# Seven buffers instead of three for the streamed hypernet matrices, and a later read-back of the first half

## The chip, the core and the metric

One core of a Trainium2 chip runs the whole program. The time is the device time of one execution in microseconds (us); the reported figure is the median of several executions. TensorE (PE in the rows) multiplies matrices, VectorE (DVE) and ScalarE (ACT) do elementwise work, GpSimd (POOL) clears memory and issues transfers here, and SyncE (SP) only issues transfers. All transfers are carried by the same 16 DMA engines, whichever engine issues them.

## What is computed

Four layers are applied to `x` (4 batches, 512 tokens, 256 features), each steered by a condition vector of 64 numbers for each batch. The second one, which the change touches, builds its weights for each batch from the condition:

```python
# layer 0: layer norm, plus tanh(cond @ lin_w.T + lin_b)
# layer 1: adapter whose weights come out of a hypernet
dWd = ((h_lang @ Wdd.T + bdd) * 0.1).reshape(B, BN, D)      # Wdd is (128*256, 64)
dWu = ((h_lang @ Wdu.T + bdu) * 0.1).reshape(B, D, BN)      # Wdu is (256*128, 64)
down = relu(einsum('bld,bnd->bln', x, Wd + dWd) + bd)
x = x + einsum('bln,bdn->bld', down, Wu + dWu) + bu
# layer 2: rms norm, up projection 256 -> 2*1024, gelu gate,
#          int8-like activations times ternary weights, residual
# layer 3: attention with 16 heads of 16, then a gated MLP 256 -> 1024 -> 256
```

`Wdd` and `Wdu` are 8 MiB each. They are read once and are by far the largest inputs.

## The kernel before

The program has a prologue, then one long body for each of the four batches. The body holds layers 2 and 3 of its batch and, tucked into its last part, layers 0 and 1 of the next. The prologue does the hypernet for all four batches together, and layers 0 and 1 of batch 0.

**The stream.** The two hypernet matrices come as 32 pieces of 512 KiB (`load(p)`, issued by SP at L268), pieces 0 to 15 from `Wdd` and 16 to 31 from `Wdu`. A piece goes into one of `PIECES` = 3 buffers in `arena`, buffer `p % 3`. Before piece p is issued, SP waits until TensorE has consumed piece p - 3 (`e_piece`). TensorE takes two pieces for each step n of 0 to 15 (`hyp(n)`, L1057, four matmuls a piece, each shown as two instructions). ScalarE scales the result of a step out of PSUM (`hyp(n)`, L452), and every second step stores it to a scratch tensor `hyp_out` in HBM (`store`, L443). `hyp(n)` on TensorE waits for ScalarE's copy of step n - 3.

**The read-back.** The result must be laid out anew, so it is fetched from `hyp_out` into `hypw`: `fetch(0)` (L279, the result of pieces 0 to 15) and `fetch(1)` (L285, pieces 16 to 31). SP issues `fetch(0)` inside the stream, right after `load(22)` (`p == 2 * (AT_DOWN - 1)` with `AT_DOWN` = 12), once the stores of pieces 0 to 15 have landed; `fetch(1)` comes after `load(31)`, when all stores have landed. VectorE adds the static weights and splits the sum into two parts (`first_weights(m)`, L774 add, L776 cast, L728 subtract).

**What sits between the pieces.** Every engine works in program order. Steps n carry other prologue work, at the same n on each engine: `parameters` after n = 1 (L1040 on TensorE), `deviation`/`front_stats`/`front_norm` at 3, `front_turn` at 4 (L1081), `weight_sum` at 6 (L1047), `first_weights(0)` at `AT_DOWN` - 1, `front_down` and `front_bottleneck` at `AT_DOWN` (six matmuls at L1071 that need `fetch(0)`). After the last piece: `first_weights(1)`, `front_up` (L1071), and then batch 0.

**GpSimd.** It clears two of the three stacked query tiles (`qst[0]`, `qst[1]`, L378) and other tiles at the start, then issues ten loads of split weights (`load_stage`, L400, 256 KiB each), four at once and each later one when VectorE has worked off the load four places before. When all pieces are consumed and all stores have landed it issues the twelve late loads (`gh_w`, `out_w`) in the same manner. `POOL_READY` = 6 counts its early clears. The query tiles are first written in the attention of batch 0, by transfers that SP issues in `stack_q`.

Of the kernel before, what the change touches and what calls it, by code (L numbers as in the profile page):

```python
# [20 lines left out]
F32 = mybir.dt.float32  # L21
# [7 lines left out]
P = 128  # L29
# [9 lines left out]
G = 4  # L39
# [13 lines left out]

HP = 8
HALF_PIECE = 256
PIECES = 3
STAGES = 4
SLOT = 2
HALF = L // 2
# [10 lines left out]
def build(nc, x, cond_t, cond_blk, vec_w, alpha_w, vecs, out_b, hyp_base, hyp_bias, hyp_w,  # L70
          up_w, down_w, qk_w, vo_w, gh_w, out_w, out):
    ctx = ExitStack()
    with ctx:
        def sb(name, shape, dt=F32):
            return ctx.enter_context(nc.sbuf_tensor(name, shape, dt))

        def sem(name):
            return ctx.enter_context(nc.semaphore(name))
# [39 lines left out]


        kst = [sb(f"kst{i}", [P, G // 2, L], F32R) for i in range(3)]  # L120
        qst = [sb(f"qst{i}", [P, G, L], F32R) for i in range(2)] + [act_both]
        inp = kst[0:2]
        vals = sb("vals", [P, T, NH, VW])
# [39 lines left out]
        oT = cut(6144, 1024, c=C, n=L)  # L163
        tmpz = fT.rearrange("p c n -> p (c n)").rearrange("p (t d) -> p t d", t=T)

        piece = cut(0, 3072, r=PIECES, g=4, n=HALF_PIECE)
        vecw_in = [x2T[0:CND, 0, :], x2T[0:CND, 1, :], vow[0:CND, 1, :]]
        down_in = hypw[:, :, :].rearrange("p b n -> p (b n)")
        bias_in = vow[:, 0, :]
# [20 lines left out]
        keys_lo_in = sem("keys_lo_in")  # L190
        keys_in = [sem(f"keys_in{i}") for i in range(3)]
        hblk_set = sem("hblk_set")
        act_zero, keys_ones = sem("act_zero"), sem("keys_ones")
        rows_in, out_done = sem("rows_in"), sem("out_done")
        pool_ready = sem("pool_ready")
# [56 lines left out]
        NPIECE = 2 * HP  # L252
        HYP_BANK = (1, 2, 7)

        AT_PARAMS, AT_STATS, AT_TURN, AT_WSUM, AT_DOWN = 1, 3, 4, 6, 12
        SMALL = 4

        block = ctx.enter_context(nc.Block())
# [2 lines left out]
        @block.sync  # L261
        def _(sp):
            def load(p):

                m, s, col = p // (2 * HP), p % (2 * HP) // 2, p % 2 * HALF_PIECE
                if p >= PIECES:
                    sp.wait_ge(e_piece, p - PIECES + 1)
                sp.dma_start(piece[:, p % PIECES, :, :],  # L268
                             hyp_w[m].rearrange("p (g s n) -> p g s n", g=4, s=HP)[:, :, s, col:col + HALF_PIECE]
                             ).then_inc(piece_in[p % PIECES], 16)  # L270

            def fetch(m):

                for hf in range(2):
                    sp.wait_ge(hyp_stored[hf], 16 * 4 * (m + 1) * HP // SLOT // 2)
                if m == 0:
                    sp.wait_ge(d_downq, 1)
                    for r in range(C):
                        sp.dma_start(hypw[:, :, r * BN:(r + 1) * BN],  # L279
                                     hyp_out[0, 4 * r:4 * r + 4, :].rearrange("b (p n) -> p b n", p=P)  # L280
                                     ).then_inc(hyp_moved, 16)
                else:
                    for first, last, moved in ((0, 1, hyp_moved), (1, B, hyp_rest)):
                        for r in range(2):
                            sp.dma_start(hypw[CND * r:CND * r + CND, first:last, D:2 * D],  # L285
                                         hyp_out[1, 4 * r + first:4 * r + last, :]
                                         .rearrange("b (p n) -> p b n", p=CND)).then_inc(moved, 16)

            sp.dma_start(hblk[:, 0:8], cond_blk).then_inc(hblk_in, 16)
            load(0)  # L290
            sp.dma_start(condT[:, :], cond_t).then_inc(params_in, 16)
            sp.dma_start(vec[:, :], vecs).then_inc(params_in, 16)
            for i in range(3):
                sp.dma_start(vecw_in[i], vec_w[:, 512 * i:512 * i + 512]).then_inc(params_in, 16)
            for p in range(1, 2 * NPIECE):
                load(p)
                if p == 2:
                    sp.dma_start(x_tok[:, :, :], x[0:L, :].rearrange("(t p) d -> p t d", p=P)
                                 ).then_inc(x_first, 16)
                if p == 4:  # L300
                    sp.dma_start(alpha[:, :], hyp_base).then_inc(small_in, 16)
                    sp.dma_start(bias_in, hyp_bias).then_inc(small_in, 16)
                if p == 6:
                    sp.dma_start(down_in, down_w).then_inc(down_sem, 16)
                if p == 8:
                    sp.dma_start(alphaw[:, :], alpha_w).then_inc(small_in, 16)
                    sp.dma_start(outb[:, :], out_b.partition_broadcast(P)).then_inc(small_in, 16)
                if p == 2 * (AT_DOWN - 1):
                    fetch(0)
            fetch(1)  # L310
            sp.wait_ge(d_base, 1)
            sp.wait_ge(e_prm, 1)
            sp.dma_start(vow[:, :, :], vo_w).then_inc(vow_in, 16)

            def stack_q(b, g):

                if g >= 3:
                    sp.wait_ge(e_score, b * (NG * T * G) + T * G * (g - 2))  # L320
                if g == 2:
                    sp.wait_ge(act_zero, b + 1)
                for e in range(2):
                    for k, part in enumerate((0, 1, 0)):
                        src = split[32 * g + DH * e:32 * g + DH * e + DH, 4 * part:4 * part + 2, :]
                        dst = qst[g % 3][32 * k + DH * e:32 * k + DH * e + DH, e::2, :]
                        sp.dma_start(dst.bitcast(F32), src.bitcast(F32)).then_inc(queries_in[e][g % 3], 16)
                    if g == 0 and e == 0:
                        sp.wait_ge(a_qk, b * 4 + 4)
                        sp.wait_ge(d_qk, b * 4 + 4)  # L330
                        sp.dma_start(keys_of(0)[64:96, :, :].bitcast(F32), split[0:32, 6:8, :].bitcast(F32)
                                     ).then_inc(keys_lo_in, 16)

            def maxima_rows(b, g):

                for k, ready in enumerate((a_mrow, d_mrow)):
                    sp.wait_ge(ready, b * NG + g + 1)
                    dst = qst[g % 3][KROWS + k:KROWS + k + 1, :, :].rearrange("p i (t n) -> p (i t) n", t=T)
                    sp.dma_start(dst.bitcast(F32), mrow[k][:, :].bitcast(F32)).then_inc(rows_in, 16)

            def batch(b, last):
                if not last:
                    sp.wait_ge(d_x3, b * T + T)
                    sp.dma_start(x_tok[:, :, :], x[bass.ds(b * L + L, L), :].rearrange("(t p) d -> p t d", p=P)
                                 ).then_inc(x_in, 16)
                sp.wait_ge(a_qk, b * 4 + 2)
                sp.wait_ge(d_qk, b * 4 + 2)
                for g in range(3):
                    stack_q(b, g)
                maxima_rows(b, 0)  # L350
                maxima_rows(b, 1)
                stack_q(b, 3)
                maxima_rows(b, 2)
                maxima_rows(b, 3)
                for h in range(2):
                    sp.wait_ge(d_outs, b * 2 + h + 1)
                    sp.dma_start(out[bass.ds(b * L + h * HALF, HALF), :].rearrange("(t p) d -> p t d", p=P),
                                 x4_tok[:, 2 * h:2 * h + 2, :]).then_inc(out_done, 16)

            with sp.Fori(0, B - 1) as b:  # L360
                batch(b, False)
            batch(B - 1, True)
            sp.wait_ge(out_done, 32 * B + 32)


        POOL_READY = 6

        @block.gpsimd
        def _(pool):
# [4 lines left out]
            for m in (ident, ident16):  # L374
                pool.affine_select(out=m[:, :], in_=m[:, :], compare_op=ALU.not_equal, fill=1.0, base=0,
                                   pattern=[[-1, P]], channel_multiplier=1).then_inc(pool_ready, 1)
            for i in range(2):
                pool.memset(qst[i][:, :, :].bitcast(F32), 0.0).then_inc(pool_ready, 1)  # L378
            pool.memset(kst[2][:, :, :].bitcast(F32), 1.0).then_inc(pool_ready, 1)
            pool.memset(vals[:, :, :, :], 1.0).then_inc(pool_ready, 1)  # L380

# [24 lines left out]
            pool.wait_ge(e_piece, 2 * NPIECE)  # L406
            for n in range(LATE, NSPLIT):
                load_stage(n)
            pool.wait_ge(pool_ready, POOL_READY)
            with pool.Fori(0, B) as b:  # L410
                pool.wait_ge(e_vg, b * 8 + 1)
# [622 lines left out]
        def _(pe):  # L1034
# [14 lines left out]
            def hyp(n):  # L1049

                if n >= 3:
                    pe.wait_ge(a_hyp, n - 2)
                for p in (2 * n, 2 * n + 1):
                    pe.wait_ge(piece_in[p % PIECES], 16 * (p // PIECES + 1))
                    col = p % 2 * HALF_PIECE
                    for g in range(4):
                        ins = pe.matmul(bank[HYP_BANK[n % 3]][32 * g:32 * g + 32, col:col + HALF_PIECE],  # L1057
                                        hblk[:, :], piece[:, p % PIECES, g, :], start=True, stop=True,
                                        tile_position=(0, 32 * g))
                    ins.then_inc(e_piece, 1)  # L1060

# [396 lines left out]
```

## Time and profile before

| | us |
|---|---|
| three executions | 771.07, 772.25, 770.39 |
| their median | 771.07 |
| profiled execution, first to last instruction | 773.6 |
| start of the last piece's matmuls | 84.29 |
| start of `front_up` | 95.21 |
| TensorE busy in the whole span | 658.1 |
| VectorE / ScalarE / GpSimd busy | 431.5 / 381.9 / 55.0 |

The profiled execution is one execution of its own; the page gives its span and no other time for it. The prologue is the first eighth of the span. In it the DMA engines are the busy resource; after it TensorE is. The profile is read from the prologue alone, since all that the change touches lies there, except a wait in `stack_q`.

### The profile page before, as it was taken

The page shows a single profiled execution, that of the slowest core. Times are in us where ns is not written, and L with a number is a line of the kernel's source. Part 1 is how long each engine was busy: PE and PEld are TensorE (multiplying, and loading weights), DVE is VectorE, ACT ScalarE, POOL GpSimd, SP SyncE. Part 2 cuts the span into 40 slices and gives each one's busy share as a digit, 9 for nine tenths or more (in the row PEclk, how much of TensorE's full clock was granted, in tenths as well). Part 3 has the DMA queues.
Part 4 walks back from the last instruction along what each step waited for, and adds up shares of the span by engine and source line. Part 5 has one row for each costly group of instructions (what it writes and reads, how often), then busy time and mean ns, then how long its engine had stood idle before and what let it go on. Part 6 is the DMA issues. An engine that isn't in the chain of part 4 may idle for free.

```text
span 773.6 us, 9912 instructions
## 1 busy us (share of the span) xinstructions
PE 658.1 (85%) x3426; PEld 436.7 (56%) x3426; DVE 431.5 (56%) x863; ACT 381.9 (49%) x729; POOL 55.0 (7%) x91
## 2 busy tenths in 40 slices
PE   2655289699989998799989998799899996999896
PEld 0411176554448876455468876354488765544585
DVE  0352078397536565588255575787165663984344
ACT  1333077426773446246863447067752554267710
POOL 4010111200000000200000000200000002000000
PEclk9755689859999999769999999689989999599999
DMA  8898521422000000502000001510000002220000
GB/s 264 292 296 285 171 87 54 95 57 44 2 1 1 1 28 28 113 13 43 2 2 1 1 28 33 118 33 11 0 0 0 14 14 62 61 44 2 1 1 28
DMA packets 34473, 44.97 MB, mean 58 GB/s; under 512 B 4736, under 2 KB 27392, under 8 KB 34304
## 3 DMA queue, kind: packets, MB, share of 16 engines
q1 hardware_dynamic: 30048, 31.87, 14.8%
q0 software_dynamic: 3872, 11.54, 5.6%
q10 hardware_dynamic: 512, 1.05, 0.4%
q8 instruction: 21, 0.34, 0.2%
q14 instruction: 20, 0.16, 0.1%
HBM read 28.45 MB, written 3.15 MB: 41 GB/s over the span
## 4 chain that ended last, share of the span: by engine, by line
PE 70%; DMA 11%; ACT 8%; DVE 6%; issue 2%; SPq 2%; ACTq 0%
PE psum L1071 31%; PE psum L1237 12%; PE psum L1257 8%; PE psum L1266 8%; DMA arena<-in_hyp_w 7%; DMA kst<-split 2%; PE psum L1057 2%; PE psum L1294 1%; DMA qst<-mrow_lo 1%; ACT arena L473 1%; ACT arena L613 1%; PE psum L1159 1%; PE psum L1090 1%; PE psum L1199 1%; PE psum L1144 1%
## 5 line engine op out<-in xcount | busy, mean ns | idle before, releaser
L916 DVE TENSOR_REDUCE mx<-psum 128x1 f32<-128x512 f32 x256 | 160.9, 683 | 48.8 <-PE psum L1237 48.4
L613 ACT ACTIVATE arena<-psum 128x512 f32<-128x512 f32 x256 | 140.8, 601 | 67.0 <-PE psum L1257 66.0
L1237 PE MATMUL psum<-kst,qst 96*128 96x512 f32 x192 | 102.9, 623 | 22.5 <-DMA kst<-split 20.7
L1071 PE MATMUL psum<-act,ghw_hi 128*128 128x512 f32 (+1 forms) x288 | 93.6, 394 | 0.5 <-DVE act L728 0.2
L1237 PEld LDWEIGHTS psum<-kst,qst 96*128 96x128 f32 x192 | 49.7, 261 | 72.4 <-DVE mx L916 41.1
L1257 PE MATMUL psum<-qst,kst 98*128 98x512 f32 x192 | 83.4, 454 | 3.6 <-DMA qst<-mrow_lo 1.8
L1071 PE MATMUL psum<-upw_hi,kst 128*128 128x512 f32 x256 | 72.2, 404 | 0.0
L1057 PE MATMUL psum<-arena,hblk 128*32 128x256 f32 x256 | 31.0, 579 | 44.3 <-DMA arena<-in_hyp_w 42.4
L1266 PE MATMUL psum<-arena,vals 128*17 128x512 f32 x512 | 67.4, 598 | 1.3 <-ACT arena L613 1.0
L1071 PEld LDWEIGHTS psum<-act,ghw_hi 128*128 128x128 f32 x288 | 56.7, 208 | 11.3 <-DVE act L728 1.7
L639 ACT ACTIVATE arena<-psum 128x512 f32<-128x512 f32 x32 | 19.2, 599 | 85.0 <-PE psum L1071 85.0
L1071 PE MATMUL psum<-act,ghw_lo 128*128 128x512 f32 (+1 forms) x144 | 55.8, 389 | 0.0
L968 DVE TENSOR_TENSOR arena<-arena,psum 128x512 f32<-128x512 f32 x32 | 22.0, 687 | 59.1 <-ACT arena L639 59.1
L1257 PEld LDWEIGHTS psum<-qst,kst 98*128 98x128 f32 x192 | 39.0, 208 | 25.5 <-ACT arena L613 16.3
L1071 PEld LDWEIGHTS psum<-upw_hi,kst 128*128 128x128 f32 x256 | 47.0, 191 | 9.6
L1071 PE MATMUL psum<-outw_hi,split 128*128 128x256 f32 x256 | 47.4, 283 | 1.2 <-DVE split L728 1.2
L551 ACT ACTIVATE arena<-psum,stat 128x512 f32<-128x512 f32 x32 | 21.9, 686 | 44.8 <-PE psum L1071 44.8
L1057 PEld LDWEIGHTS psum<-arena,hblk 128*32 128x32 f32 x256 | 6.8, 135 | 65.5 <-DMA arena<-in_hyp_w 38.3
L1071 PEld LDWEIGHTS psum<-outw_hi,split 128*128 128x128 f32 x256 | 41.2, 188 | 4.6 <-DVE split L728 2.1
L390 POOL DMA_DIRECT2D kst<-split x44 | 21.3, 490 | 273.4 <-ACT split L577 154.7
L1071 PE MATMUL psum<-upw_lo,kst 128*128 128x512 f32 x128 | 40.2, 395 | 0.0
L928 DVE RECIPROCAL rden<-psum 128x16 f32<-128x16 f32 (+1 forms) x20 | 4.7, 234 | 59.5 <-PE psum L1278 59.5
(162 smaller groups left out, 1025.2 us busy)
## 6 DMA issues: line engine op xcount, KB each, us to landing
arena<-in_hyp_w SPq DMA_DIRECT2D x32, 512.0 KB, 5.2
kst<-split POOLq DMA_DIRECT2D x44, 128.0 KB, 4.0
qst<-split SPq DMA_DIRECT2D x72, 64.0 KB, 3.4
arena<-in_x SPq DMA_DIRECT2D x4, 512.0 KB, 3.5
arena<-in_up_w POOLq DMA_DIRECT2D x8, 256.0 KB, 7.7
arena<-in_gh_w POOLq DMA_DIRECT2D x8, 256.0 KB, 3.8
out_x<-arena SPq DMA_DIRECT2D x8, 256.0 KB, 2.1
act<-split SPq DMA_DIRECT2D x24, 64.0 KB, 2.3
```

What stands on the lines that cost most here:

```text
L390: pool.dma_start(keys_of(g)[32 * k:32 * k + 32, :, :].bitcast(F32), src.bitcast(F32)).then_inc(keys_in[g % 3], 16)
L473: s.activation(to, src(c), ACT.Identity, scale=scale, bias=prm[:, col_b + c:col_b + c + 1]).then_inc(signal, 1)
L551: s.activation(gl[:, n % 2, :], bank[2 * (n % 2) + 1], ACT.Gelu, scale=stat[:, RS2, t:t + 1]).then_inc(a_gelu, 1)
L613: s.activation(probs[:, kb % 2, i, :], bank[3 + n % RING], ACT.Exp).then_inc(a_p, 1)
L639: s.activation(sg[:, f % 2, :], bank[2 * (f % 2)], ACT.Silu).then_inc(a_silu, 1)
L916: v.reduce_max(mx[:, g % 2, col:col + 1], bank[u % RING], AX.X).then_inc(d_max, 1)
L968: v.tensor_tensor(hh[:, f % 2, :], sg[:, f % 2, :], bank[2 * (f % 2) + 1], ALU.mult).then_inc(d_hh, 1)
L1057: ins = pe.matmul(bank[HYP_BANK[n % 3]][32 * g:32 * g + 32, col:col + HALF_PIECE], hblk[:, :], piece[:, p % PIECES, g, :], start=True, sto ...
L1071: ins = pe.matmul(dst, lhs(a, c), rhs(z, c), start=start and n == 0, stop=stop and n == len(terms) - 1, skip_group_check=skip)
L1237: pe.matmul(bank[u % RING], qst[g % 3][0:KROWS, i, P * t:P * t + P], keys_of(g)[0:KROWS, i // 2, :], start=True, stop=True).then_inc(e_max, 1)
L1257: pe.matmul(bank[3 + k % RING], keys_of(g)[0:SROWS, i // 2, P * kb:P * kb + P], qst[g % 3][0:SROWS, i, :], start=True, stop=True).then_inc ...
L1266: ins = pe.matmul(bank[6][32 * i:32 * i + VW, :], vals[:, kb, G * g + i, :], probs[:, kb % 2, i, :], start=(kb == 0), stop=(kb == T - 1), ...
```

## The change

The ring of piece buffers grows from 3 to 7. Three stay where they were, in `arena`. The other four lie in a tensor `early_pieces` whose memory is given back at once and is then allocated again as `qst[0]` and `qst[1]`. These two tiles can therefore be cleared only after the last piece is consumed: GpSimd clears them after the fourth late weight load, a new semaphore `queries_zero` tells SP, and `stack_q` waits for it before the first stacked queries of each batch. `AT_DOWN` goes from 12 to 13, and `fetch(0)` is issued after `load(24)`.

```diff
-PIECES = 3
+PIECES = 7
+ARENA_PIECES = 3
...
+        with nc.sbuf_tensor("early_pieces", [P, 2 * G * L], F32) as early_pieces:
+            pass
         qst = [sb(f"qst{i}", [P, G, L], F32R) for i in range(2)] + [act_both]
...
-        piece = cut(0, 3072, r=PIECES, g=4, n=HALF_PIECE)
+        arena_piece = cut(0, 1024 * ARENA_PIECES, r=ARENA_PIECES, g=4, n=HALF_PIECE)
+        early_piece = early_pieces[:, :].rearrange("p (r g n) -> p r g n", g=4, n=HALF_PIECE)
+
+        def piece(p):
+            r = p % PIECES
+            return arena_piece[:, r, :, :] if r < ARENA_PIECES else early_piece[:, r - ARENA_PIECES, :, :]
...
-        AT_PARAMS, AT_STATS, AT_TURN, AT_WSUM, AT_DOWN = 1, 3, 4, 6, 12
+        AT_PARAMS, AT_STATS, AT_TURN, AT_WSUM, AT_DOWN = 1, 3, 4, 6, 13
...
                 if p >= PIECES:
                     sp.wait_ge(e_piece, p - PIECES + 1)
-                sp.dma_start(piece[:, p % PIECES, :, :],
+                sp.dma_start(piece(p),
...
-                if p == 2 * (AT_DOWN - 1):
+                if p == 24:
                     fetch(0)
...
+                if g == 0:
+                    sp.wait_ge(queries_zero, 2)
                 if g >= 3:
                     sp.wait_ge(e_score, b * (NG * T * G) + T * G * (g - 2))
...
-        POOL_READY = 6
+        POOL_READY = 4
...
-            for i in range(2):
-                pool.memset(qst[i][:, :, :].bitcast(F32), 0.0).then_inc(pool_ready, 1)
             pool.memset(kst[2][:, :, :].bitcast(F32), 1.0).then_inc(pool_ready, 1)
...
             for n in range(LATE, NSPLIT):
                 load_stage(n)
+                if n == LATE + STAGES - 1:
+                    for i in range(2):
+                        pool.memset(qst[i][:, :, :].bitcast(F32), 0.0).then_inc(queries_zero, 1)
```

How the instructions stand. SP, from the ninth piece to the last transfer of the prologue (`in_hyp_w` is a piece, `hypw<-hyp_out 128x4x128` is `fetch(0)`). Before:

```order
L306 DMA alphaw<-in_alpha_w 64x512
L307 DMA outb<-in_out_b 128x256
L268 DMA arena<-in_hyp_w 128x4x256 x14
L279 DMA hypw<-hyp_out 128x4x128 x2
L268 DMA arena<-in_hyp_w 128x4x256 x9
L285 DMA hypw<-hyp_out 64x256 x2
L285 DMA hypw<-hyp_out 64x3x256 x2
L313 DMA vow<-in_vo_w 128x1024
```

After:

```order
L278 DMA arena<-in_hyp_w 128x4x256
L278 DMA early_pieces<-in_hyp_w 128x4x256 x4
L278 DMA arena<-in_hyp_w 128x4x256 x3
L278 DMA early_pieces<-in_hyp_w 128x4x256 x4
L278 DMA arena<-in_hyp_w 128x4x256 x3
L278 DMA early_pieces<-in_hyp_w 128x4x256
L289 DMA hypw<-hyp_out 128x4x128 x2
L278 DMA early_pieces<-in_hyp_w 128x4x256 x3
L278 DMA arena<-in_hyp_w 128x4x256 x3
L278 DMA early_pieces<-in_hyp_w 128x4x256
L295 DMA hypw<-hyp_out 64x256 x2
L295 DMA hypw<-hyp_out 64x3x256 x2
```

Nine pieces stood behind `fetch(0)`, and seven stand there now.

TensorE, from the pieces behind `front_turn` to `front_up` (`kst,split` x6 is `front_down`, `split` x6 is `front_up`; a piece is `x4`). Before:

```order
L1057 MATMUL psum<-arena,hblk 32x256 x16
L1047 MATMUL psum<-wstat,alpha_ob 128x1
L1057 MATMUL psum<-arena,hblk 32x256 x48
L1071 MATMUL psum<-kst,split 128x512 x6
L1057 MATMUL psum<-arena,hblk 32x256 x24
L1071 MATMUL psum<-split 128x512 x6
```

After:

```order
L1070 MATMUL psum<-early_pieces,hblk 32x256 x16
L1060 MATMUL psum<-wstat,alpha_ob 128x1
L1070 MATMUL psum<-arena,hblk 32x256 x12
L1070 MATMUL psum<-early_pieces,hblk 32x256 x16
L1070 MATMUL psum<-arena,hblk 32x256 x12
L1070 MATMUL psum<-early_pieces,hblk 32x256 x16
L1084 MATMUL psum<-kst,split 128x512 x6
L1070 MATMUL psum<-arena,hblk 32x256 x12
L1070 MATMUL psum<-early_pieces,hblk 32x256 x4
L1084 MATMUL psum<-split 128x512 x6
```

Six pieces stood behind `front_down`, and four stand there now.

GpSimd, from its early clears to the last late load. Before:

```order
L378 MEMSET qst 128x2048 x2
L379 MEMSET kst 128x1024
L380 MEMSET vals 128x1088
L400 DMA arena<-in_up_w 128x512 x8
L400 DMA arena<-in_qk_w 128x512 x2
L400 DMA arena<-in_gh_w 128x512 x8
L400 DMA arena<-in_out_w 128x512 x4
```

After:

```order
L389 MEMSET kst 128x1024
L390 MEMSET vals 128x1088
L410 DMA arena<-in_up_w 128x512 x8
L410 DMA arena<-in_qk_w 128x512 x2
L410 DMA arena<-in_gh_w 128x512 x4
L421 MEMSET qst 128x2048 x2
L410 DMA arena<-in_gh_w 128x512 x4
L410 DMA arena<-in_out_w 128x512 x4
```

The two clears moved from the front of the queue to behind the fourth late load.

## Rows read from the trace of the kernel before

**Rows 1.** The head of the page: the span.
```profile
span 773.6 us, 9912 instructions
```

**Rows 2.** Windows: length, busy us (instructions) by engine, clock, DMA share, GB/s.
```profile
7.00:25.00 18.00, 9.04 (x56) 6.20 (x60) 0.09 (x1) 2.90 (x5) 2.49 (x5) 1.00 1.01 343
25.00:28.00 3.00, 2.13 (x20) 0.59 (x12) 2.43 (x16) 1.11 (x2) 0.00 (x0) 1.00 0.45 145
28.00:36.00 8.00, 2.11 (x20) 0.59 (x24) 4.14 (x17) 2.70 (x4) 0.54 (x1) 0.68 0.97 329
36.00:42.00 6.00, 4.76 (x36) 2.08 (x32) 2.52 (x5) 4.50 (x7) 0.54 (x1) 0.58 0.72 237
42.00:51.00 9.00, 3.67 (x34) 0.96 (x33) 7.53 (x9) 2.34 (x4) 2.48 (x3) 0.64 1.02 329
51.00:61.00 10.00, 5.40 (x40) 1.10 (x40) 0.69 (x1) 1.74 (x4) 0.54 (x1) 0.50 0.78 247
61.00:70.00 9.00, 3.51 (x28) 0.86 (x32) 2.53 (x5) 2.28 (x4) 0.00 (x0) 0.50 1.03 336
70.00:72.00 2.00, 1.50 (x16) 0.20 (x8) 0.00 (x0) 0.32 (x2) 0.00 (x0) 0.50 0.66 179
76.00:84.00 8.00, 2.76 (x32) 0.60 (x28) 1.29 (x2) 2.16 (x4) 0.00 (x0) 0.88 0.71 232
```

**Rows 3.** Waits of SP's queue up to 100 us: total us, times, longest.
```profile
SPq L268 <- PE psum L1057: 48.1, 24, 6.0
```

**Rows 4.** Timeline: start, us, engine; three pieces of TensorE's other work between the pieces.
```profile
19.13 3.58 PE L1040 MATMUL psum<-condT,arena 64*128 64x4 f32 x16
...
36.62 1.97 PE L1081 MATMUL psum<-ident,arena 128*128 128x128 f32 x8
...
72.33 2.93 PE L1071 MATMUL psum<-kst,split 128*128 128x512 f32 x6
```

**Rows 5.** Timeline: piece 15, the stores behind it, and `fetch(0)`.
```profile
47.27 1.08 PE L1057 MATMUL psum<-arena,hblk 128*32 128x256 f32 x8 [0.49 <-DMA arena<-in_hyp_w]
...
49.05 1.32 ACTq L443 DMA_DIRECT2D hyp_out<-arena  x4
...
58.76 1.95 SPq L279 DMA_DIRECT2D hypw<-hyp_out  x2
```

**Rows 6.** The chain that ended last, in order of time: piece 28, piece 31 to `front_up`.
```profile
77.58 0.67 PE psum L1057 x8
...
84.29 1.12 PE psum L1057 x8
...
87.06 2.06 DMA hyp_out<-arena
...
89.71 4.21 DMA hypw<-hyp_out
...
94.40 0.30 DVE split L776
...
95.21 2.94 PE psum L1071 x6
```

**Rows 7.** Timeline: GpSimd's clears and loads, and a VectorE pass beside one.
```profile
1.88 3.54 POOL L378 MEMSET qst<- 128x2048 f32 x2
...
46.46 1.41 POOL L400 DMA_DIRECT2D arena<-in_qk_w  x1 [0.76 <-DVE upw_lo L725]
46.47 1.29 DVE L701 TENSOR_SCALAR hypw<-hypw,wstat 128x2048 f32<-128x2048 f32 x1
...
89.65 2.12 POOL L400 DMA_DIRECT2D arena<-in_gh_w  x4 [31.56 <-DMA hyp_out<-arena]
```

**Rows 8.** Instructions that write or read `hypw`: times; min/median/max ns; forms.
```profile
L728 DVE TENSOR_TENSOR split<-hypw,split x5: 426/692/693, 67.8 to 575.7; 128x512 fp32r<-128x512 f32 x3, 128x256 fp32r<-128x256 f32 x2
...
L765 DVE CAST split<-hypw x3: 420/423/423, 239.5 to 575.2; 128x512 fp32r x2, 128x512 fp32r<-128x512 f32 x1
```

**Rows 9.** Transfers by issue, whole span: number, KB each, median us to landing.
```profile
arena<-in_up_w POOLq DMA_DIRECT2D x8, 256.0 KB, 7.7
```

More of the change, by code:

```diff
@@ L192, in build @@
         hblk_set = sem("hblk_set")
+        queries_zero = sem("queries_zero")
         act_zero, keys_ones = sem("act_zero"), sem("keys_ones")
@@ L1057, in hyp @@
                         ins = pe.matmul(bank[HYP_BANK[n % 3]][32 * g:32 * g + 32, col:col + HALF_PIECE],
-                                        hblk[:, :], piece[:, p % PIECES, g, :], start=True, stop=True,
+                                        hblk[:, :], piece(p)[:, g, :], start=True, stop=True,
                                         tile_position=(0, 32 * g))
```

## The prediction

> **What bounds the kernel now.** The change lives in the prologue, so I read the chain of waits from `front_up` backwards, then the windows over the stream, then what TensorE did in each window where the DMA engines were not full.
>
> The chain [rows 6] shows a fixed tail. The last piece's matmuls start at 84.29, its copy is stored (the store lands after 2.06 us), `fetch(1)` takes 4.21 us, and `front_up` starts at 95.21. The tail of 95.21 - 84.29 = 10.9 us contains no choice that the ring of buffers could touch; it follows wherever the last piece lands. Everything behind `front_up` (batch 0, the late loads, the other batches) starts from it. So the question is only when piece 31 lands.
>
> The windows [rows 2] tell what paces the stream. The DMA engines have two kinds of stretches. In 7:25, 28:36, 42:51 and 61:70 they are full (share 0.97 to 1.03) and move 329 to 343 GB/s. In 25:28, 36:42, 51:61, 70:72 and 76:84 they are partly empty (0.45, 0.72, 0.78, 0.66, 0.71) and move 145 to 247 GB/s. TensorE is busy for 3.51 of the 9 us in 61:70, with the DMA engines full, so it paces nothing by its own throughput. What it does is to hold buffers: SP's queue waited 48.1 us in 24 waits on TensorE's pieces [rows 3], so SP is nearly always waiting for a free buffer. Whenever TensorE turns to something else, at most two further pieces are in flight and the DMA engines run dry: the parameter matmuls from 19.13 (one of two groups, 3.58 us) stand ahead of 25:28, the transposes at 36.62 (1.97 us, and the wait for their input) in 36:42, and `front_down` at 72.33 (2.93 us) ahead of 76:84 [rows 4]. In 51:61 `fetch(0)`, issued at 58.76 [rows 5], stands in SP's queue between two pieces.
>
> **The change part by part.**
>
> *Seven buffers: the holes fill.* The five hollow stretches last 3 + 6 + 10 + 2 + 8 = 29 us. By bytes they moved 0.435 + 1.422 + 2.470 + 0.358 + 1.856 = 6.54 MB; at the 332 GB/s of the full stretches (between 329 and 336 [rows 2]; 7:25 holds other inputs too) that is 19.7 us, so 9.3 us go. By busy share they used 1.35 + 4.32 + 7.80 + 1.32 + 5.68 = 20.5 us, so 8.5 us go. I take 8.9 us, with both ends.
>
> Does a depth of seven really cover every hole? A piece takes 524 KB / 332 GB/s = 1.6 us of full DMA time, so seven stand for 11 us of work. The longest hold is the one at step 4, where TensorE waits for the normalised input and then transposes; it is no longer than the 6 us of the hollow stretch around it, 36:42 [rows 2]. The parameters hold it for about 5 us. Six us eat not quite four pieces, and three are still in flight: the cover holds, with some 5 us to spare.
>
> *A deeper queue does not cost rate.* In 7:25 the input x, the biases and GpSimd's first weight loads were queued beside the pieces, more than in any later stretch, and it was the fastest one (343 GB/s) [rows 2]. From there the cost is nothing; the bound on the other side is that 343 holds throughout, which is in the last rival.
>
> *`fetch(0)` after `load(24)`.* SP stops in it until the stores of pieces 0 to 15 have landed; queued behind it are loads 25 to 31. Piece 15 starts at 47.27 and its store is issued from 49.05 to 50.4 [rows 5]. When it lands there is not shown: 2.06 us later if it goes as the last store [rows 6], and no later than 58.76, when `fetch(0)` was issued. So SP is free between 5 and 11.5 us after piece 15's start. `load(24)` goes out when piece 17 is consumed, about 4 us after it; at that time pieces 18 to 24 are out, 11 us of work. Even the late end leaves about 3 us of queued pieces. Cost nothing; bound 1 us. The fetch then stands behind piece 24, and its reader `front_down` behind piece 27, three pieces or 4.8 us later, against about 1.2 us of VectorE work between: covered.
>
> *`front_down` after piece 27.* Its 2.93 us [rows 4] now come when four pieces are still to be taken. They land 1.6, 3.2, 4.8 and 6.4 us after piece 27, whether TensorE is busy or not. TensorE is back 4 us after piece 27 landed, and takes a piece in 0.67 us (piece 28, right after `front_down`) to 1.12 us (piece 31) [rows 6]. At 0.67 the backlog is gone when piece 31 lands; at 1.12 it ends 1.1 us late. I take 0.2.
>
> *GpSimd's clears leave the start.* Its first loads go out 3.5 us earlier [rows 7]. The DMA engines have spare share only before 7 us, some tenths of a us. I take it at nothing, gain bound 0.5.
>
> *The clears arrive at the tail.* GpSimd is released for the late loads with SP's `fetch(1)`: four issues from 89.65 last 2.12 us, to 91.8; two clears of 1.77 us each [rows 7] would stand at 91.8 to 95.3. The fifth late load waits for VectorE and went out far later, so no load is delayed. But VectorE's cast of the last weights starts at 94.40 [rows 6], in the second clear, on the tail. Do the two disturb each other? The trace has one such meeting: a load issue on GpSimd that takes 0.53 us elsewhere took 1.41 us beside a VectorE pass of 1.29 us, and ended just after it [rows 7]. That pass ran at 0.63 ns an element; the cast runs at 0.83 (423 ns for 512), where the subtraction takes 1.35 (692 ns) [rows 8]: both belong to the fast kind. No row shows a clear that starts first, so the bounds are 0 and 95.3 - 94.4 = 0.9 us. I take 0.9, since the nearest row shows that one waits for the other's end.
>
> The Trainium skill (SBUF — State Buffer, on the shared port pair) says that GpSimd and a VectorE copy or cast in its two-port mode exclude each other for whole instructions, whoever starts first. By that rule this is a cost of 0.9 us; without it the sum would be 0.9 us better. The trace agrees in the other order only (1.41 us in place of 0.53).
>
> *The wait on `queries_zero`.* Set at about 95 us, first asked for in the attention near 145: nothing.
>
> The sum: -8.9 + 0.2 + 0.9 = -7.8 us, nearly all of it before `front_up`. On the profiled span that is 773.6 [rows 1] to 765.8. The span lies 2.5 us above the median of the three executions; the edit is the same in both, so the forecast is 771.07 - 7.8 = 763.3 us, a gain of 1.0%.
>
> **The rivals.**
>
> *Only part of the holes closes* (something other than the buffers holds the stream). TensorE's step waits for ScalarE's copy three steps back, ScalarE in its order waits for the weight loads, and these took 7.7 us to land beside the stream [rows 9]. If more pieces ahead stretch them beyond the lead of four steps, some 18 us (16 steps in about 74 us), ScalarE holds TensorE and the ring fills up all the same. For it: the loads share the 16 engines. Against it: the 7.7 us were measured with the engines full most of the time. It would leave the holes of 36:42 and 51:61, or 1.7 + 2.2 us by share, so a gain of 7.8 - 3.9 = 3.9: 767.2 us.
>
> *The holes don't close at all* (the share dips because of small packets or HBM, not for lack of transfers). Then time stays at 771 plus or minus 1. Against it: each hole follows a hold of TensorE.
>
> *Slower: the read-back comes too late.* Stores on ScalarE's queue must get through beside seven pieces. If they land late, SP stands in `fetch(0)` with loads 25 to 31 behind it, and `front_down` on TensorE waits for the fetch with pieces 28 to 31 behind it. It starts to cost when the store behind piece 15 needs more than some 12 us (11 us of queued pieces), and each us more is a us. To eat the 7.8 us it must take over 20 us, where the trace bounds it by 9.7. At 24 us: 775 us.
>
> *More comes back*: the rate of 7:25 (343) holds through, no clash at the cast, 10.5 us: 760.6.
>
> **How the numbers follow.** The forecast of 763.3 with its ends (holes 8.5 to 9.3, cast 0 to 0.9, `front_down` 0 to 1.1, `fetch(0)` 0 to 1, start 0 to -0.5, and the drift of the rest of the program of about 1 us between executions) covers 761.2 to 766.5 and gets 0.67. More comes back 0.09. Part of the holes 0.13. Nothing 0.06. Slower 0.05. The range for 8 in 10 is 760.8 to 767.8. A measurement of this kernel tells about 0.2%, or 1.5 us, from no change. Faster by over 0.2%: 0.67 + 0.09 + 0.13 = 0.89, less a little for a partial gain under 1.5 us, 0.88. Within it 0.07. Slower 0.05.
>
> **What would show it.** In the profile of the changed kernel the windows up to the last piece should read 0.95 or more throughout, with SP's waits still long (the ring is full, not empty). The last piece's matmuls should start near 75.5 and `front_up` near 87.3. `fetch(0)` should be issued and no window behind it should dip. The cast of the second half should start late or stand beside the second clear. If the last piece is early but the time is not, something behind `front_up` took its place. If it is not early, look for who TensorE waited for in the stream: ScalarE's copies (first rival) or the fetch (third).

## Result and profile after

| | before | after |
|---|---|---|
| median of the executions, us | 770.73 (4) | 759.35 (4) |
| lowest to highest | 768.83 to 772.25 | 756.47 to 759.86 |
| ratio, 95% interval | | 0.9844 (0.9821 to 0.9868) |
| profiled span | 773.6 | 757.1 |
| last piece's matmuls start | 84.29 | 70.33 |
| `front_up` starts | 95.21 | 81.55 |

The change made the kernel 11.4 us faster by the medians, 12.0 by the ratio. The forecast was 763.3 us, a gain of 7.8, with a range of 760.8 to 767.8. The measured time lies below that range: the sign and the mechanism were right, the size was too small. The same kernel, measured twice more beside other experiments, came out at 0.9834 (0.9809 to 0.9858) and 0.9843 (0.9819 to 0.9867) of the kernel before.

First the windows over the stream, the counterpart of [rows 2]: length, busy us and instructions of TensorE, its weight loads, VectorE, ScalarE, GpSimd, then granted clock, DMA share and GB/s.

```profile
7.00:23.00 16.00, 8.71 (x52) 6.00 (x56) 0.00 (x0) 2.70 (x5) 0.00 (x0) 1.00 1.06 381
23.00:46.00 23.00, 14.86 (x114) 4.76 (x106) 16.71 (x43) 10.65 (x19) 3.56 (x5) 0.84 1.07 369
46.00:56.00 10.00, 6.25 (x48) 1.30 (x48) 2.08 (x3) 3.46 (x6) 0.54 (x1) 0.50 1.07 365
56.00:65.00 9.00, 4.74 (x40) 1.03 (x40) 2.44 (x5) 2.34 (x4) 0.00 (x0) 0.50 1.00 333
65.00:70.00 5.00, 5.00 (x34) 2.60 (x34) 0.00 (x0) 1.79 (x3) 0.00 (x0) 0.56 0.80 270
```

Two things are to be seen. The hollow stretches are gone: none of these windows up to 65 reads under 1.00, and in windows of 2 us between 8 and 68 the lowest share is 0.97. (In the two later profiles of the same kernel the lowest were 0.94 and 0.92, both at 62:64.) And the full stretches are fuller than before: 365 to 381 GB/s at a share of 1.06 to 1.07 up to 56 us, where the full stretches of before moved 329 to 343 at 0.97 to 1.03 [rows 2]. The second goes beyond the prediction, whose last rival had 343 throughout.

SP's queue waited far less for TensorE than in [rows 3] (48.1 us); instead its issues got longer. The row of the waits of SP's queue (total, times, longest), and the row of the pieces into the new memory (shortest, median, longest issue in ns), where the median before was 540:

```profile
SPq L278 <- PE psum L1070: 16.8, 18, 1.9
...
L278 SPq DMA_DIRECT2D early_pieces<-in_hyp_w x17: 546/1587/2438, 7.9 to 61.2; - x17
```

The chain that ended last, from `front_down` to `front_up`, answers to [rows 6]:

```profile
65.91 2.86 PE psum L1084 x6
68.77 2.22 PE psum L1070 x32
71.01 0.61 ACT arena L465
...
75.27 3.83 DMA hypw<-hyp_out
...
79.58 1.47 DVE split L789
...
81.55 2.94 PE psum L1084 x6
```

The tail keeps its length (70.33 to 81.55 is 11.2 us, before 10.9), but two of its steps are new in kind. The last four pieces (x32; the last of them from 70.33) run back to back right behind `front_down`: they had all but landed while TensorE was busy with it. And the cast at L789 takes 1.47 us in place of 0.30. The timeline shows what stands beside it:

```profile
75.21 2.12 POOL L410 DMA_DIRECT2D arena<-in_gh_w  x4 [24.99 <-DMA hyp_out<-arena]
...
77.32 3.56 POOL L421 MEMSET qst<- 128x2048 f32 x2
79.12 0.42 DVE L787 TENSOR_TENSOR hypw<-hypw,alpha 128x256 f32<-128x256 f32 x1 [8.35 <-DMA hypw<-hyp_out]
79.58 1.45 DVE L789 CAST split<-hypw 128x256 fp32r<-128x256 f32 x1
```

The second clear runs from 79.10 to 77.32 + 3.56 = 80.88, and the cast ends at 81.03. The add just before it (L787) also ran beside that clear, in its usual 0.42 us: only the cast was held up.

`front_up` starts 13.7 us earlier than before, while the medians differ by 11.4 and the two spans by 16.5. What lies behind `front_up` is the same work in both, and its length differs by some us from execution to execution: 678.4 us in the profile of before, 675.6 in that of after, 674.5 to 677.9 in the ten other profiles below. A span lies 1.8 us under the time of its execution in every run here, so the profiled execution of before took about 775.4 us, more than any of its times in the table. The pair of spans therefore overstates the gain, its 84.29 and 95.21 may be late as well, and the ratio of the times is the figure to keep. In two further profiles of the changed kernel `front_up` started at 82.02 and 83.17, 13.2 and 12.0 us earlier than in the one profile of before.

### The profile page after: what moved, and what is told of

The parts are those of the page before. It is cut to its first block, busy times and chain, and to the rows that moved or that the text cites. A ratio compares the mean times of both kernels' runs of the same rounds, so it can differ in the third digit from the quotient of the medians.

```text
span 757.1 us, 9912 instructions
## 1 busy us (share of the span) xinstructions
PE 655.9 (87%) x3426; PEld 434.2 (57%) x3426; DVE 432.2 (57%) x863; ACT 381.4 (50%) x729; POOL 55.0 (7%) x91
## 3 DMA queue, kind: packets, MB, share of 16 engines
q10 hardware_dynamic: 512, 1.05, 0.4%
## 4 chain that ended last, share of the span: by engine, by line
PE 69%; DMA 12%; ACT 8%; DVE 6%; SPq 3%; issue 2%; ACTq 0%
PE psum L1084 31%; PE psum L1250 12%; PE psum L1270 8%; PE psum L1279 8%; DMA early_pieces<-in_hyp_w 5%; DMA kst<-split 2%; PE psum L1307 1%; DMA qst<-split 1%; DMA arena<-in_hyp_w 1%; SPq L339 1%; DMA qst<-mrow_lo 1%; ACT arena L486 1%; ACT arena L626 1%; PE psum L1172 1%; PE psum L1103 1%
## 5 line engine op out<-in xcount | busy, mean ns | idle before, releaser
L929 DVE TENSOR_REDUCE mx<-psum 128x1 f32<-128x512 f32 x256 | 160.5, 681 | 48.1 <-PE psum L1250 47.6
L1084 PE MATMUL psum<-act,ghw_hi 128*128 128x512 f32 (+1 forms) x288 | 91.1, 386 | 1.2 <-DVE act L741 0.8
L1084 PEld LDWEIGHTS psum<-act,ghw_hi 128*128 128x128 f32 x288 | 54.6, 199 | 12.0 <-DVE act L741 2.5
L871 DVE SCALAR_TENSOR_TENSOR arena<-psum,stat,arena 128x512 f32<-128x512 f32 x32 | 23.9, 748 | 21.7 <-ACT arena L564 21.6
L1084 PE MATMUL psum<-outw_lo,split 128*128 128x256 f32 x128 | 36.1, 282 | 0.0
```

What stands on the lines that cost most here:

```text
L871: v.scalar_tensor_tensor(hbuf[:, t % 2, 512 * j:512 * j + 512], bank[2 * (n % 2)], stat[:, RS2, t:t + 1], gl[:, n % 2, :], ALU.mult, ALU.m ...
L929: v.reduce_max(mx[:, g % 2, col:col + 1], bank[u % RING], AX.X).then_inc(d_max, 1)
L1084: ins = pe.matmul(dst, lhs(a, c), rhs(z, c), start=start and n == 0, stop=stop and n == len(terms) - 1, skip_group_check=skip)
```

## Experiments

### What sets the rate: the stream alone

SP loads pieces and nothing else runs. The kernel leaves out the whole computation; its output is a copy of `x`.

```python
for d in (1, 2, 3, 4, 5, 7):                # buffers in the ring
    for p in range(16):
        if p >= d:
            sp.wait_ge(sems[d][p % d], 16 * (p // d))     # piece p - d has landed
        sp.dma_start(rings[d][:, p % d, :, :], <piece p>).then_inc(sems[d][p % d], 16)
    <wait until all have landed>
```

> This kernel computes nothing: SP alone loads pieces of the hypernet matrix, in six sections of 16 pieces, with rings of 1, 2, 3, 4, 5 and 7 buffers (tensors ring1 to ring7). A piece is issued when the piece that held its buffer before has landed; no engine reads them. The output is only a copy of x. Theory 'depth' (a deeper queue moves more bytes a second): about 4.0 us for a piece at depth 1 (130 GB/s), 2.1 at 2, 1.6 at 3 (330 GB/s), 1.45 at 4, 1.40 at 5 (375), and no more at 7. Rival 'other inputs' (the higher rate after the change comes from what runs beside the pieces or where they land): depths 3 to 7 all the same within 3%.

The windows inside the six sections, in the order of the depths (the last two numbers are DMA share and GB/s):

```profile
5.00:60.00 55.00, 0.00 (x0) 1.00 0.44 137
65.00:93.00 28.00, 0.00 (x0) 1.00 0.79 257
99.00:123.00 24.00, 0.00 (x0) 1.00 1.02 329
128.00:150.00 22.00, 0.00 (x0) 1.00 1.10 351
155.00:177.00 22.00, 0.00 (x0) 1.00 1.07 346
183.00:205.00 22.00, 0.00 (x0) 1.00 1.07 345
```

With three pieces out and no engine holding a buffer, the stream moves 329 GB/s at a share of 1.02. That is what the full stretches of the kernel before looked like. With four it moves 351 at 1.10, and five or seven bring no more. So a share of 1.0 is not the top: three transfers of 512 KiB keep the DMA engines short by some 6%. The expectation was right up to depth 4 and too high at five (375 against 346). The rival, no difference from 3 to 7, falls: 3 and 4 differ by 7%.

This leaves open why the changed kernel ran at 365 to 381.

### A second queue beside the stream

The same pieces, rings of 3 and of 7, each once alone and once with GpSimd loading ten 256 KiB weight tiles beside them. Again nothing is computed.

```python
SECTIONS = ((3, 0), (3, 10), (7, 0), (7, 10))     # (buffers, weight loads on GpSimd)
pool.dma_start(side[k][:, p % 4, :], up_w[:, c, n:n + 512])     # four in flight
```

> Computes nothing, output a copy of x: four sections of 16 pieces by SP alone, ring of 3 buffers, ring of 3 with GpSimd loading ten 256 KiB weight tiles (2 KiB runs) beside it, ring of 7, ring of 7 with the same loads. stream_alone levelled off at 345 to 351 GB/s from depth 4, while the changed kernel ran at 365 to 381. Theory 'several queues': a second issuing queue raises the level, 365 to 380 GB/s at depth 7 with the loads, 345 to 350 without; at depth 3, 330 without and 345 or more with. Rival 'the level differs by stage': no difference with and without the loads.

Windows: ring of 3 alone, ring of 3 with the loads, ring of 7 alone, ring of 7 after its loads had ended.

```profile
6.00:28.00 22.00, 0.00 (x0) 1.00 1.00 323
...
36.00:46.00 10.00, 2.69 (x5) 1.00 1.06 372
...
76.00:88.00 12.00, 0.00 (x0) 1.00 1.10 349
110.00:124.00 14.00, 0.00 (x0) 1.00 1.10 348
```

With the loads beside it even the ring of 3 moves 372 GB/s in 36:46 (expected were 345 or more), and 349 over 32:46, its slow first windows included, against 323 alone. The ring of 7 had its loads out from about 94 to 110; the 2 us windows of that stretch read 287 and 224 GB/s up to 98, then 394, 370, 362, 374, 363 and 360, and 348 to 349 as soon as the loads were through. So for a ring of 3 the loads raise the rate. For a ring of 7 the level is 348 for pieces alone and 360 to 394, in the mean 370, with weight loads of 2 KiB runs among the pieces of 1 KiB runs, but only after the slow start: over 94:110 as a whole it is 342, no more than alone. The run doesn't tell whether it is the second queue, the longer runs or, for the ring of 3, simply more transfers out that lifts it. The changed kernel held 369 over 23:46 with loads in the mix; this run doesn't show why it could hold that for so long. In the kernel before the same loads ran beside the pieces in 42:51 and the rate was 329; that TensorE held one of its three buffers for part of that time is a likely reason, not a tested one.

### Seven buffers, but fewer pieces out

```diff
                 if p >= PIECES:
-                    sp.wait_ge(e_piece, p - PIECES + 1)
+                if p >= FLIGHT:
+                    sp.wait_ge(e_piece, p - FLIGHT + 1)
```

(The first line goes with the second.) `FLIGHT` is 3, 5 and 4 in the three kernels; everything else is as in the changed kernel.

> The changed kernel with its seven buffers, but SP issues piece p only when piece p - 3 is consumed, so at most three are out, as before the change. Theory 'depth': the full stretches fall back to about 332 GB/s and the holes come back; the last piece's matmuls start near 84, front_up near 95.3, time 770 to 772. Rival 'place' (other memory, clears gone from the start, later fetch): the full stretches keep 365 GB/s and more; last piece near 78, time near 765.

> The changed kernel with seven buffers and at most five pieces out. Holes theory (what counts is to bridge TensorE's other work): a piece takes 1.5 us, five bridge 7.5 us, so the longest hold of 5 to 6 us is just covered and nearly all of the gain stays: last piece's matmuls at 71 to 72.5. Rate theory (each further piece in the queue raises the rate): it ends between, near 74 to 76. Time 760 to 762 by the first, 763 to 765 by the second.

> Seven buffers, at most four pieces out. The stream alone is as fast at four as at seven, and four pieces bridge 4 x 1.45 = 5.8 us, about the longest hold. Theory 'rate saturates at four': last piece's matmuls at 71 to 73, time 759 to 761.5. Rival 'bridging needs more than four': 74 to 77, time 763 to 766.

| pieces out | window 23:46, share and GB/s | ScalarE's last copy of the stream | `front_up` | time against before, 95% |
|---|---|---|---|---|
| 3 | 0.77, 244 | 86.57 | 97.1 | 1.0001 (0.9976 to 1.0027) |
| 4 | 0.97, 322 | 74.72 | 85.25 | 0.9876 (0.9848 to 0.9905) |
| 5 | 1.05, 358 | 71.42 | 81.97 | 0.9856 (0.9812 to 0.9900) |
| 7 | 1.07, 369 | 71.01 | 81.55 | 0.9844 (0.9821 to 0.9868) |

The window 23:46 of the kernel before and then of three and of four pieces out; with four, also three short windows, behind the parameters, between the holes and behind the transposes:

```profile
23.00:46.00 23.00, 12.82 (x101) 5.75 (x105) 12.58 (x38) 10.47 (x18) 2.14 (x4) 0.74 0.85 290
```

```profile
23.00:46.00 23.00, 10.80 (x80) 3.87 (x72) 11.44 (x37) 9.11 (x16) 1.07 (x2) 1.00 0.77 244
```

```profile
23.00:46.00 23.00, 14.12 (x110) 4.66 (x102) 16.16 (x43) 10.65 (x17) 3.56 (x5) 0.86 0.97 322
26.00:28.00 2.00, 1.07 (x12) 0.23 (x8) 1.86 (x10) 0.60 (x1) 0.54 (x1) 1.00 0.81 253
32.00:36.00 4.00, 3.56 (x24) 1.77 (x16) 1.76 (x4) 2.79 (x5) 0.54 (x1) 1.00 1.07 376
42.00:44.00 2.00, 1.08 (x8) 0.20 (x8) 1.90 (x5) 0.42 (x1) 1.41 (x1) 0.50 0.86 268
```

With three pieces out the whole gain is gone, though the pieces lie in the new memory, the clears have left the start and `fetch(0)` comes later. The rival 'place' falls: the gain is that of the number of pieces out, and nothing else in the change brings any that the times resolve (0.9976 to 1.0027). Four bring most of it, and five cannot be told from seven: the time of 760.19 is within what was expected, the last piece (70.71) a little before it. For four the last piece was expected at 71 to 73 and came at 74.04, as the rival had it; the time, 760.95, fell into the theory's 759 to 761.5. The stream alone was as fast at four as at seven, but here TensorE keeps one piece, or several, while it works, and 23:46 reads 0.97. The short windows show where: 0.81 behind the parameters and 0.86 behind the transposes, where seven pieces out read 1.10 and 1.12. Between the holes (32:36) four moved 376 GB/s and seven 380. So four pieces are too few to bridge TensorE's other work. Whether a lower rate adds to that stays open: 44:48 moved 302 GB/s with four, 356 with seven.

### The clears in GpSimd's gap

```diff
-            for i in range(2):
-                pool.wait_ge(hyp_stored[i], 16 * 4 * NPIECE // SLOT // 2)
             pool.wait_ge(e_piece, 2 * NPIECE)
+            for i in range(2):
+                pool.memset(qst[i][:, :, :].bitcast(F32), 0.0).then_inc(queries_zero, 1)
+            for i in range(2):
+                pool.wait_ge(hyp_stored[i], 16 * 4 * NPIECE // SLOT // 2)
             for n in range(LATE, NSPLIT):
                 load_stage(n)
-                if n == LATE + STAGES - 1:
-                    for i in range(2):
-                        pool.memset(qst[i][:, :, :].bitcast(F32), 0.0).then_inc(queries_zero, 1)
```

> The changed kernel with the two clears of the query tiles moved ahead of GpSimd's wait for the stores (still behind its wait for the last piece). Theory 'clash': the cast of the second half of the weights, 1.45 us after the change and 0.29 before it, is back at 0.29 us, and front_up starts 1.2 us earlier against the last piece's matmuls (10.0 to 10.1 us behind them in place of 11.2). Time 1.2 us less than the changed kernel, near 758. Rival: the cast is long for another reason (weight loads being issued beside it) and stays above 1 us.

> The kernel of clears_in_gap once more, now beside the changed kernel itself. Theory 'clash': 1.2 us less than the changed kernel (about 0.15%), so the medians lie 1 to 1.5 us apart. Rival: the 1.2 us saved at the cast are lost again behind front_up, and the two agree within 0.5 us.

The timeline of the second of these two runs, GpSimd and VectorE at the tail:

```profile
71.67 3.54 POOL L416 MEMSET qst<- 128x2048 f32 x2 [21.32 <-PE psum L1069]
75.85 2.12 POOL L410 DMA_DIRECT2D arena<-in_gh_w  x4 [0.63 <-issue]
...
80.09 0.29 DVE L788 CAST split<-hypw 128x256 fp32r<-128x256 f32 x1
```

The clears now end before the stores have landed, and the cast is back at 0.29 us, so the clash is shown, and the rival (weight loads being issued beside the cast) falls, since these end before the cast in both kernels. `front_up` starts at 80.89 and 80.90, against 81.55 and, on the same chip, 82.02 for the changed kernel. On the clock of the whole program the gain is under what can be told: 0.9822 (0.9796 to 0.9848) beside 0.9834 (0.9809 to 0.9858), medians 756.15 and 757.09. The first of the two runs had no changed kernel beside it: 758.16, 0.9834 (0.9787 to 0.9882).

### The place of the fetch and of `front_down`

Seven buffers with the old place, and three buffers with the new one:

```diff
-        AT_PARAMS, AT_STATS, AT_TURN, AT_WSUM, AT_DOWN = 1, 3, 4, 6, 13
+        AT_PARAMS, AT_STATS, AT_TURN, AT_WSUM, AT_DOWN = 1, 3, 4, 6, 12
-                if p == 24:
+                if p == 22:
                     fetch(0)
```

```diff
-        AT_PARAMS, AT_STATS, AT_TURN, AT_WSUM, AT_DOWN = 1, 3, 4, 6, 12
+        AT_PARAMS, AT_STATS, AT_TURN, AT_WSUM, AT_DOWN = 1, 3, 4, 6, 13
```

(The second is made on the kernel before, whose fetch follows `AT_DOWN`.)

> The changed kernel as it is, beside the next three on the same chip, to have a common base. Last piece's matmuls near 70.3, front_up near 81.5, time 758 to 760.

> The changed kernel with its seven buffers and moved clears, but fetch(0) after load(22) and front_down after piece 25 again, as before the change. My prediction took the move for free, bound 1 us. Theory 'free': last piece's matmuls at 70 to 71.5, time 758.5 to 760.5. Rival 'the move matters': SP reaches fetch(0) before the stores of pieces 0 to 15 have landed and stands there, the windows behind it dip under 0.9, last piece 1 to 3 us later, time 760 to 762.

> The kernel before with three buffers and clears at the start, but fetch(0) after load(24) and front_down after piece 27. If the later fetch matters by itself it shows here: theory 'free' gives the last piece's matmuls at 83.5 to 85 and the time of the kernel before within 1 us; the rival gives 2 us less or more.

Seven buffers, fetch after load(22): the chain, windows behind the fetch, which was issued from 49.59 on, and SP's wait in front of it.

```profile
69.91 0.68 PE psum L1070 x8
70.62 0.61 ACT arena L465
```

```profile
50.00:52.00 2.00, 1.49 (x13) 0.43 (x16) 0.00 (x0) 0.60 (x1) 0.00 (x0) 1.00 0.89 281
...
58.00:66.00 8.00, 6.94 (x51) 2.97 (x54) 0.74 (x2) 3.03 (x6) 0.00 (x0) 1.00 1.09 385
```

```profile
SPq L287 <- DMA hyp_out<-arena: 2.8, 1, 2.8
```

The first half of the rival came about. SP reached the fetch before the stores had landed and stood there for 2.8 us (2.6 in the kernel with both edits below), which it does not in the changed kernel, and 50:52 dips to 0.89. But the ring bridged it: the last copy stands at 70.62, the changed kernel's at 71.01 and 71.46, and the time is 758.61, 0.9854 (0.9822 to 0.9887). So the old place costs no time that can be told with seven buffers.

The windows show one thing more. From 58 to 66 this kernel moved 385 GB/s, though the last weight load had been issued at 49.42 and VectorE was at work on the fetched half from 56.73: only pieces and four small stores were on their way. The stream alone, which read the first half of the matrix only, stayed at 348. So weight loads are not the only thing that goes with a rate above 350, and what else does was not tested.

Three buffers with the new place measured 770.37, 1.0010 (0.9991 to 1.0030), no change, though in its profile the last piece came at 82.27, 2 us earlier than before. That profile is nearer to the rival than to 'free'; the times are not, and one profile each is too little to tell 2 us of a three-deep stream (the kernel with seven buffers and three out had its last piece at 85.42). The later fetch is no part of the gain.

### Both edits together

The clears in the gap, and fetch and `front_down` at their old places, beside the changed kernel.

> The changed kernel once more, as the base beside the next one. front_up near 82.0, time 757 to 760.

> Seven buffers, clears in GpSimd's gap, and fetch(0) after load(22) with front_down after piece 25. The traces of the two edits apart had front_up at 80.9 (clears) and 81.3 (fetch), where the changed kernel has 81.6 to 82.0. Theory 'front_down after piece 27 stands in the way of the last four pieces' (they run back to back behind it and the last ends 0.9 us late): front_up at 79.8 to 80.2, time 2 us under the changed kernel, 755 to 757. Rival: the two gains overlap and front_up stays at 80.7 or later.

Its chain:

```profile
70.41 0.61 ACT arena L464
...
80.04 2.94 PE psum L1083 x6
```

`front_up` starts at 80.04, where theory put it, and 3.1 us before the changed kernel's on the same chip (83.17). Its median is 757.48, a little over the 755 to 757 expected, beside 758.87, but the ratios to the kernel before, 0.9841 (0.9817 to 0.9866) and 0.9843 (0.9819 to 0.9867), are the same. The traces favour both edits: the cast is short again in all three profiles with the clears in the gap, and the last copy is at 70.41 and 70.62 with the old place against 71.01 to 72.62 in five profiles with the new one. The time of the whole program does not resolve it.

## Why the prediction missed the size

**Holes close, -8.9 us: the right mechanism, and the mis-sized term.** The last piece's matmuls came 84.29 - 70.33 = 14.0 us earlier (12.4 and 13.5 in the two further profiles of the changed kernel, all against one profile of before, whose execution took longer than the others). The step that failed is the reading that the stretches with a share of 0.97 to 1.03 are full, at 332 GB/s, with the sentence after it that a deeper queue leaves the rate as it is. The stream alone shows 329 GB/s at 1.02 with three out and 351 at 1.10 with four, and the changed kernel ran at 369. Redone with the 369 of 23:46, which [rows 2] did not give: the 6.54 MB of the hollow stretches take 17.7 us instead of 29, so 11.3 go. The other 48 us between 7 and 76 moved 16.1 MB (with 72:76 at 331) and would take 43.7, so 4.3 more go. That is 15.6; with the 351 of the stream alone it would be 10.4 + 2.1 = 12.5. The last 14 us of the new stream run at 333 and 270 GB/s, 0.82 MB less than at 369, which takes 2.2 us back, and the first 16 us at 381 give 0.5: some 14 us, as seen. All of this is an estimate.

Part of it was no matter of rate. In shorter windows of the kernel before, the "full" stretches are averages over small holes and fuller pieces:

```profile
14.00:20.00 6.00, 1.88 (x12) 1.07 (x13) 0.00 (x0) 0.60 (x1) 0.00 (x0) 1.00 1.04 386
...
30.00:32.00 2.00, 0.25 (x7) 0.23 (x8) 0.14 (x3) 0.60 (x1) 0.00 (x0) 0.71 0.84 263
32.00:36.00 4.00, 1.23 (x12) 0.20 (x8) 2.14 (x7) 2.10 (x3) 0.00 (x0) 0.50 1.04 365
...
72.00:76.00 4.00, 3.95 (x22) 2.12 (x22) 0.69 (x1) 1.66 (x4) 0.00 (x0) 0.60 1.01 331
```

These could have warned: 365 and 386 GB/s had been reached with three buffers, the second with other inputs queued beside the pieces, so 332 was no level of the engines. I read 7:25 as 'no loss from a deeper queue' and its mean of 343 as the end of a rival (343 throughout, 760.6), where it held 386 for 6 us. How the 14 us split between small holes and a higher rate was not measured.

**Cover for seven buffers.** Right. The share is at 0.97 or above in every 2 us through the parameters and the transposes, and even five pieces out were enough. The sign that went with it, waits of SP that stay long, did not show: 16.8 us in place of 48.1, with longer issues.

**`fetch(0)` after `load(24)`, 0.** Right: it was issued at 50.29, 0.1 us after `load(24)`, so SP did not stand in it. The third rival, the late read-back, did not come about, nor did the stop of ScalarE on the weight loads; these landed in 5.6 us (median), faster than the 7.7 of [rows 9].

**`front_down` after piece 27, 0.2.** A little low. It became the releaser of the last four pieces. With it two pieces earlier the last copy stood at 70.62 and 70.41, with it in its new place at 71.01 to 72.62 in five profiles of the same stream, 0.4 to 2.2 us later.

**The clash at the cast, 0.9.** Right in place and kind, 1.16 us by size (1.45 against 0.29; the cast took 1.15 to 1.74 in the six other profiles with the clears in that place), and shown by moving the clears. The Trainium skill (SBUF — State Buffer, section "SBUF: two separate sides") says that whoever starts first holds the shared pair of ports for its whole instruction. The trace before agreed for VectorE first (1.41 us in place of 0.53); this one agrees for GpSimd first, the cast ending 0.15 us behind the clear.

**Clears gone from the start, 0.** The first weight loads were issued at 3.72 instead of 7.21; the last piece with three out (85.42) shows no gain from it.

**From the profile to the time.** The forecast carried a shift of `front_up` over one to one. It moved by 12.0 to 13.7 us in three profiles, the time by 11.4 to 12.8; within the scatter that holds.

## What to carry to other kernels

The ring in front of a streamed load has two jobs, to bridge the reader's other work and to keep enough transfers out, and the buffer that the reader holds counts for neither. Before calling a stretch full, read it again in windows of 2 to 6 us, and look whether those with the most transfers out are faster than the rest; if so, price a deeper ring with more than the holes. Here the time with five 512 KiB pieces out could not be told from that with seven. And when a clear or copy is moved to another engine's idle time, look at which idle time: GpSimd had a gap of 4 us right before the place where its clears met the cast.

## What the hardware showed beyond expectation

The DMA share of the windows goes above 1.0 and its top is not 1.0: 1.02 at 329 GB/s, 1.10 at 348 to 351. One queue of pieces with 1 KiB runs, alone, levels off at about 350 GB/s from four transfers out on; in one kernel the pieces moved 385 GB/s for 8 us, and the reason is open. Weight loads of 2 KiB runs issued by GpSimd beside it went with 372 against 323 for a ring of three, and for a ring of seven with 370 against 348 once under way, though over the whole stretch with loads out only with 342. With seven pieces out the issue itself gets longer on SP, 1.59 us in the median against 0.54 (1.42 in the stream alone); with five out it was still 0.54 in both. SP then stands in the issue rather than in the wait, and the rate is no lower for it.
